# Two buffers for the offset rows, a split turn of the features, taps divided by pair, and a bank sum in one VectorE operation

## What is computed

```
off1 = make_offset(conv3x3(x, tm1_w, tm1_b), conv3x3(x, tr1_w, tr1_b))
out  = relu(batchnorm(deform_conv(x, off1, dcn1_w), bn1_g, bn1_b))
off2 = make_offset(conv3x3(out, tm2_w, tm2_b), conv3x3(out, tr2_w, tr2_b))
out  = batchnorm(deform_conv(out, off2, dcn2_w), bn2_g, bn2_b)
return relu(out + x)
```

## Time and profile before

| | |
|---|---|
| median of 3 runs | 425.51 us (425.49 to 426.92) |
| profiled execution | 425.25 us, of which the traced span is 423.4 us |
| PE busy | 395.9 us, 94% of the span |
| ACT busy | 326.9 us, 77% |
| DVE busy | 312.6 us, 74% |
| POOL busy | 105.3 us, 25% |
| granted TensorE clock | 0.99 in the mean |

### The profile page before, as it was taken

How to read it: one execution, slowest core, us unless ns; L and a number is a source line. 1 busy time by engine, 2 the same in 40 slices (tenths; PEclk the granted TensorE clock), 3 DMA queues, 4 the chain that set the end, 5 groups by cost and what they waited for, 6 DMA issues and landing times.

```text
span 423.4 us, 19117 instructions
## 1 busy us (share of the span) xinstructions
PE 395.9 (94%) x7747; PEld 354.7 (84%) x7747; DVE 312.6 (74%) x868; ACT 326.9 (77%) x423; POOL 105.3 (25%) x229
## 2 busy tenths in 40 slices
PE   4878999999999999999998899999999999999980
PEld 4666789999999999999885788999999898998870
DVE  4658977778887777777438888877777777777435
ACT  2627878888888898888836878888888889888745
POOL 6203413333333222229001422222111222220000
PEclk9999999999999999999999999999999999999996
DMA  7301422221122222222001331222222222222005
GB/s 227 80 2 36 83 56 52 49 43 35 34 41 46 45 45 45 48 50 41 2 3 26 60 65 35 50 45 45 45 45 48 47 47 48 49 49 40 4 2 198
DMA packets 61433, 21.28 MB, mean 50 GB/s; under 512 B 53702, under 2 KB 61212, under 8 KB 61388
## 3 DMA queue, kind: packets, MB, share of 16 engines
q1 hardware_dynamic: 56876, 18.34, 20.3%
q0 software_dynamic: 4512, 2.30, 2.1%
HBM read 3.23 MB, written 2.10 MB: 13 GB/s over the span
## 4 chain that ended last, share of the span: by engine, by line
PE 87%; DVE 5%; ACT 2%; DMA 2%; issue 1%; SPq 1%; DVEq 0%; ACTq 0%
PE acc_ps L759 56%; PE z_ps L732 12%; PE build_ps L717 9%; PE side_ps L665 3%; PE acc_ps L783 3%; PE side_ps L654 2%; DMA xs<-in_x 1%; ACT raw L576 1%; PE acc_ps L611 1%; PE build_ps L601 1%; DMA moved<-conv_sb 1%; DVE bstats L891 1%; PE acc_ps L643 1%; SPq L291 1%; ACT S L495 1%
## 5 line engine op out<-in xcount | busy, mean ns | idle before, releaser
L759 PE MATMUL acc_ps<-S,Z 64*64 64x256 f32 x4416 | 279.2, 377 | 1.7 <-issue 0.9
L759 PEld LDWEIGHTS acc_ps<-S,Z 64*64 64x64 f32 x4416 | 223.8, 133 | 20.8 <-issue 3.6
L495 ACT ACTIVATE S<-build_ps,minus 128x1024 f32<-128x1024 f32 x190 | 201.4, 1112 | 29.2 <-PE build_ps L717 28.9
L732 PE MATMUL z_ps<-wz,xflat 64*64 64x192 f32 x1536 | 106.7, 328 | 0.0
L717 PE MATMUL build_ps<-feat_rows,cst 64*64 64x512 f16 x576 | 82.5, 377 | 2.3 <-ACT S L495 1.2
L488 ACT ACTIVATE Z<-z_ps 128x768 f32<-128x768 f32 x96 | 78.2, 814 | 4.9 <-PE z_ps L732 4.9
L732 PEld LDWEIGHTS z_ps<-wz,xflat 64*64 64x64 f32 x1536 | 75.5, 132 | 6.7 <-issue 1.3
L1020 DVE TENSOR_SCALAR S<-build_ps 128x512 f32<-128x512 f32 x96 | 66.0, 688 | 17.3 <-PE build_ps L717 16.1
L291 POOL DMA_DIRECT2D moved<-conv_sb x128 | 64.9, 514 | 18.1 <-POOL conv_sb L384 15.8
L1022 DVE TENSOR_SCALAR S<-build_ps 128x512 f32<-128x512 f32 x96 | 65.3, 680 | 0.0
L384 POOL TENSOR_TENSOR conv_sb<-conv_sb,cst 128x32 f32<-128x32 f32 x28 | 7.5, 268 | 205.7 <-ACT conv_sb L482 205.7
(11 more groups left out here) (116 smaller groups left out, 305.1 us busy)
## 6 DMA issues: line engine op xcount, KB each, us to landing
xs<-in_x SPq DMA_DIRECT2D x4, 512.0 KB, 6.6
out<-raw SPq DMA_DIRECT2D x7, 256.0 KB, 2.5
moved<-conv_sb SPq DMA_DIRECT2D x56, 11.2 KB
moved<-conv_sb POOLq DMA_DIRECT2D x56, 11.3 KB, 1.6
moved<-conv_sb POOLq DMA_DIRECT2D x44, 11.2 KB, 1.6
wz<-in_dcn_w POOLq DMA_DIRECT2D x2, 288.0 KB, 4.7
feat_rows<-feats SPq DMA_TRANSPOSE x32, 3.7
moved<-conv_sb SPq DMA_DIRECT2D x28, 12.0 KB
```

The lines of the kernel that those rows point to most:

```text
L495: act.activation(S[:, (parity + b) % 2, half, 0:ACT_TAPS, :], build_ps[:, 0:ACT_TAPS, :], ACT.Relu, bias=minus2[:, :], scale=1.0 if half = ...
L732: mm = pe.matmul(z_ps[halves[c], i, h * BLOCK_COLS:(h + 1) * BLOCK_COLS], xflat[parity][halves[i], pixels], wz[halves[i], layer, h, b * BL ...
L759: mm = pe.matmul(acc_ps[halves[i], g, 0:HW], Z[halves[g], slot, i, half, j * C:(j + 1) * C], S[halves[g], slot, half, j, :].rearrange(by_i ...
```

## The change

Five edits, on all engines:

- `conv_sb` and `moved` become two buffers each, chosen by the pair's parity, with semaphores of their own; the waits that `shift` and `copy_taps` of pair index 3 had (`after_places`, `after_shift`) go. On ACT that `copy_taps` moves ahead of `copy_Z(T, 2)` in index 0, and `pad(T + 4)` moves behind `rectify(T, 2)`.
- The taps are divided between SP and POOL anew: of pair index 2 SP moves four and POOL five, of index 3 two and seven, of all others five and four.
- The features of the pair with index 1 are turned by two transfers, four slices and then eight, with semaphores of their own; PE's `build` of that pair's block 0 waits for the first alone, and stands after two steps of `sample(T, 0, 2)` and not after four.
- `keep_sums` on DVE is one operation, which adds `lower_sums` to `acc_ps` bank 0; `upper_kept` goes, and `sample(T, 0)` on PE waits for `raw_ready`.
- The statistics of a layer's first pair are taken in index 14 and not in index 1.

```diff
-SP_TAPS = (4, 1, 7, 3)
-POOL_TAPS = (0, 2, 5, 6, 8)
-LATE_SP_TAPS, LATE_POOL_TAPS = SP_TAPS + POOL_TAPS[4:], POOL_TAPS[:4]
-EARLY_PAIRS = 4
+TAP_ORDER = (4, 1, 7, 3, 8, 5, 6, 2, 0)
+SP_TAPS_OF_FIRST, SP_TAPS_OF_OTHERS = (4, 2), 5
...
-        conv_sb = sb("conv_sb", [P, HW])
-        moved = sb("moved", [P, HW])
+        conv_sb = [sb(f"conv_sb{i}", [P, HW]) for i in range(2)]
+        moved = [sb(f"moved{i}", [P, HW]) for i in range(2)]
...
-                turn_feats(first, 0, SLICES)
-                shift(first + 2, layer)
-                turn_feats(first + 1, 1)
+                turn_feats(first, 0, slice(SLICES, SLICE_BLOCKS))
+                shift(first + 2, 0, layer)
+                turn_feats(first + 1, 1, slice(0, SLICES), second_turned)
+                turn_feats(first + 1, 1, slice(SLICES, SLICE_BLOCKS))
...
-            def shift(T, layer, after_places=False):
+            def shift(T, parity, layer):
...
-                if after_places:
-                    pool.wait_ge(places_done, T)
-                move_taps(pool, LATE_POOL_TAPS if is_late(T, layer) else POOL_TAPS, shifted_by_pool)
+                move_taps(pool, parity, TAP_ORDER[:taps_by_sp(T, parity, layer) - 1:-1], shifted_by_pool)
...
                     rectify(T, parity, 1)
                     if index == 0:
+                        copy_taps(T + 3, 1 - parity, layer, T + 2)
                         copy_Z(T, parity, 2)
+                        rectify(T, parity, 2)
                         pad(T + 4, parity, T + 4 - first, layer)
-                        copy_taps(T + 3, layer, True)
-                        rectify(T, parity, 2)
...
                 if b == 0:
-                    wait(pe, upper_kept, T)
-                    wait(pe, lower_kept, T)
+                    wait(pe, raw_ready, T)
...
-                    places_of_taps(T + 2, layer)
-                    sample(T, 0, 2, range(4))
-                    build(T + 1, 1, 0, layer)
+                    places_of_taps(T + 2, 0, layer)
+                    sample(T, 0, 2, range(2))
+                    build(T + 1, 1, 0, layer, second=True)
                     weigh(T + 1, 1, 0, layer)
-                    sample(T, 0, 2, range(4, 6))
+                    sample(T, 0, 2, range(2, 6))
...
             def keep_sums(T, t):
                 wait(dve, sampled, BLOCKS * (T + 1))
-                dve.tensor_copy(raw[:, t, :], acc_ps[:, 0, 0:HW]).then_inc(upper_kept, 1)
-                wait(dve, upper_kept, T + 1)
                 wait(dve, lower_kept, T + 1)
-                dve.tensor_tensor(raw[:, t, :], raw[:, t, :], lower_sums[:, :], ALU.add).then_inc(raw_ready, 1)
+                dve.tensor_tensor(raw[:, t, :], acc_ps[:, 0, 0:HW], lower_sums[:, :], ALU.add).then_inc(raw_ready, 1)
...
-                    statistics(T - 1, T - 1 - first)
+                    if index != 1:
+                        statistics(T - 1, T - 1 - first)
+                    if index == PAIRS - 2:
+                        statistics(first, 0)
```

More of the change, by code:

```diff
@@ L284, in program, with move_taps @@
         turned_ps = (acc_ps[:, 0, 0:2 * P], acc_ps[:, 1, 0:2 * P])
-        def move_taps(eng, taps, shifted):
+        def move_taps(eng, parity, taps, shifted):
             for k in taps:
@@ L416, in body @@
                     if index < PAIRS - 3:
-                        shift(T + 3, layer, index == 0)
+                        shift(T + 3, 1 - parity, layer)
                     if 0 < index < PAIRS - 2:
@@ L538, in _ @@
                 rectify_first_half(first)
-                copy_taps(first + 2, layer)
+                copy_taps(first + 2, 0, layer)
                 rectify(first, 0, 0, (1,))
@@ L700, in places, with build @@
                 mm.then_inc(places_done, 1)
-            def build(T, parity, b, layer, is_first=False, products=range(6)):
+            def build(T, parity, b, layer, is_first=False, products=range(6), second=False):
                 if products[0] == 0:
@@ L707, in build @@
                         wait(pe, rows_by_dve, layer + 1)
-                    elif b == (1 if is_first else 0):
+                    elif b == 0 and second:
+                        wait(pe, second_turned, 16 * (layer + 1))
+                    elif b == (1 if is_first or second else 0):
                         wait(pe, feats_turned, turned(T))
@@ L836, in body @@
                         conv_taps(T + 3, 1 - parity, layer, T + 1)
-                    build(T, parity, 1, layer, products=range(4))
+                    build(T, parity, 1, layer, products=range(4), second=index == 1)
                     if index is None or index < PAIRS - 2:
-                        places_of_taps(T + 2, layer)
+                        places_of_taps(T + 2, parity, layer)
                     build(T, parity, 1, layer, products=range(4, 6))
@@ L996, in features @@
                             wait(dve, first_turned, layer + 1)
+                        if isinstance(T, int) and T == layer * PAIRS + 2:
+                            wait(dve, second_turned, 16 * (layer + 1))
                         ins = dve.tensor_tensor(taken[:, :, :, ROW_CODES],
```

114 lines of the change are left out of this document (58 added, 56 removed).

## The result

The changed kernel takes 431.99 us in the median of six runs (431.37 to 434.65), the kernel before 425.87 us on the same chip (six runs). The ratio of the two is 1.0141, with a 95% interval of 1.0107 to 1.0175: about 6.0 us slower (4.6 to 7.5). The forecast was 3.8 us slower. Two executions count as slow and stand outside the ratios of this document: one of the kernel before at 430.68 us, beside `raw_last` and `stats_early`, and one of `kept_last` at 1921.63 us.

The account below looks back on a forecast made before the run. PE, busy 395.9 of 423.4 us, was taken to bound the kernel. Loop pairs 4.0, written-out pairs 1.0 and layer start -1.2 gave +3.8 us: 429.3 us, forecast band 427.5 to 431.5, range 424.2 to 435.0.

Parts of the forecast that it names:

- Loop pairs: Heads of the twenty loop pairs: PE's sampling starts later behind the one-operation sum, 0.2 us a pair, +4.0 us (0 to +8.0).
- the last quarter would sample from 96.25 to 96.33 and lose 0.07 to 0.15: Odd loop pair's head: PE's last quarter, free of weighing at 96.18, waits for the load at 96.25.
- Written-out pairs: Eight pairs, indices 12 to 15 of each layer: 0.05 us for 12 and 13, 0.2 for 14 and 15, +1.0 us.
- Start of a layer: Second pair's sampling starts earlier, limited by DVE's features: -0.98 us in layer 1, -0.2 in layer 0, together -1.2.
- Statistics, tap shares, second buffers at nothing: Moved statistics, new SP and POOL shares, and extra loads and memset at the program's head were forecast to cost nothing.
- Rival 1: At pair heads the whole array waits for the first product: 0.40 us a loop pair, +10.0, 435.5 us; chance 0.22.
- Rival 2: The wait at pair heads is absorbed: -1.2, 424.3 us, chance 0.14; 423.5 and below, chance 0.06.
- Rival 3: Layer start gains nothing, as POOL's taps land late or two transfers hold SP up: +5.0, 430.5 us; chance 0.08.
- the spacing: Sign: equal pieces of PE's chain of waits lie 11.3 to 11.6 us a pair apart instead of 11.24.
- the earlier second sampling: Sign: PE's first sampling product of the second pair comes about 1 us earlier in layer 1, about 0.2 in layer 0.
- The addition's delay of 0.04 to 0.13 us: Sign: DVE's addition starts that long after the end of ACT's `lower_sums`.
- PE's list of waits: Sign: PE waits for DVE's `raw` line, 0.1 to 0.3 us each, some 30 times.

Follow-up runs that it names:

- raw_last: Changed kernel without VectorE's redundant wait for the sampling, and TensorE waits for Z and S first, the sum last: 429.69 us, ratio to before 1.0080.
- stats_early: Changed kernel with the first pair's statistics put back to the second pair: 433.46 us, ratio to before 1.0165.
- kept_last: `two_ops` with TensorE waiting for Z and S first and for the two bank copies last: 425.72 us, ratio to before 0.9983.
- bank1_first: Changed kernel with a pair's first sampling product taken on bank 1 ahead of bank 0, bank 1 waiting for ScalarE's copy alone: 432.60 us, ratio to before 1.0121.
- one_wait_less: Changed kernel without VectorE's own wait for the sampling ahead of the addition: 431.35 us, ratio to before 1.0143.
- one_op_alone: Kernel before with the bank sum in one operation and nothing else of the change: 433.24 us, ratio to before 1.0189.
- sum_twice: Changed kernel with the bank sum's addition made twice in a row, TensorE waiting for the second: 446.12 us, ratio to before 1.0446.
- two_ops: Changed kernel with the bank sum put back to two operations, copy then addition, all else kept: 424.57 us, ratio to before 0.9987.

## Why the prediction was right, and where its sizes were not

The sign and the range held; the forecast's own band, 427.5 to 431.5 us, was just missed, since the loss was larger than forecast. Term by term, beside the 7.0 us of the stage table:

- **Loop pairs: forecast +4.0 (0 to 8.0), measured +6.1.** The mechanism, a price near what the last quarter loses, is what `bank1_first` and the table of quarters show. The step that was mis-sized is "the last quarter would sample from 96.25 to 96.33 and lose 0.07 to 0.15": it lost 0.22 us in this odd pair (1.11 to 1.33) and 0.32 in an even one (1.03 to 1.35); the pairs lost 0.24 and 0.34. Three things went into it. The addition came 0.21 to 0.23 us behind the copy, not 0.13: I took the delay of a wait on one of two inputs from the earlier trace rows, and the new wait stands with a second one ahead of an operation whose address is made in the loop (`one_wait_less` takes 0.07 off). PE's step was 0.21, a little under my 0.25. And from the first product to the last quarter's start it is another 0.07 us, which I left out. I also read the last quarter's freedom in the odd pair alone; in the even one it had begun earlier.
- **Written-out pairs: forecast +1.0, measured +1.7.** Index 12 lost 0.04 (forecast 0.05), index 14 0.26 (forecast 0.2: its last quarter started at 0.86 before and at 1.13 after). The rest is index 13: it took 10.94 us before and 11.28 after, though its last quarter started at 1.11 and 1.13. I put it with 12 and measured it by its last quarter; but in it the first two quarters count, and those went from 0.78 to 1.12, just the 0.34 that the pair lost.
- **Start of a layer: forecast -1.2, measured -0.85** (way to head 1 and pair 1 together: -0.16 in layer 0, -0.69 in layer 1). My figure held the new sum at head 1, and so does this one. The mechanism came: what is late next is DVE with the features of pair index 2, the addition of head 1 starts 0.64 us behind ACT's copy, and PE waits 0.27 us for it. That PE samples 0.98 us earlier in layer 1 and 0.2 in layer 0 came out as 1.3 and 0.4, reckoned from each layer's start. What I left out is what pair 1 gives back behind that: 0.57 us in layer 1 and 0.29 in layer 0, from its first sampling product to head 2; the unnamed stall in layer 0 is 0.49 us where it was 0.29, and one of 0.18 us came in layer 1; the rest is open. Beside the one-operation sum the other parts are worth 1.9 us by the stage table (`one_op_alone` against the changed kernel; 2.0 by their times), of which 0.68 is a difference in layer 1's way to head 1 that single executions can't tell; beside two operations they are worth some 0.5.
- **Statistics, tap shares, second buffers at nothing:** no row speaks against it for the statistics and the loop's shares. At the start of layer 0 PE now waits 0.33 us for the shifted rows of pair index 3, where it had not waited before; the last of SP's two taps landed at 49.28 and of POOL's seven at 49.09. Shares and buffers were not tried alone.
- **Rivals.** Rival 1 at 0.40 a pair: falls with `bank1_first`, although the total lies between it and the forecast. Rival 2: falls with `sum_twice` and `one_op_alone`. Rival 3: both waits of the earlier trace rows are gone in the changed kernel, but the 0.8 us hung on a late landing, and `two_ops` has waits of 0.47 and 0.72 us for the shifted rows at the same places of the two layers; so it falls beside the one-operation sum only, and beside two operations most of it holds.

Of the signs I had named, the spacing (11.50 and 11.56 us, within 11.3 to 11.6) and the earlier second sampling came. The addition's delay of 0.04 to 0.13 us was wrong in the loop (0.21 to 0.23), a wait for `moved` remained, and PE's list of waits did not show the wait some 30 times but twice; a sign that can be read only in the timeline was the wrong one to name. No version beat the kernel before by more than the uncertainty: `two_ops` and `kept_last` are 0.1 to 0.2% ahead, with 1.0 at the edge of both intervals.

## What to carry to other kernels

An operation saved on an engine that waits saves nothing; if the saving turns two parallel releases into a chain, the whole chain is paid at every place where the next engine has no slack. On an array split in quarters, look for the quarter whose work ends last, which here was mostly the one that starts last, and measure the new chain against that one, for every parity of the loop and every kind of pair. And price a chain by its waits as well as by its operations: here 0.42 us of addition came with 0.42 us of steps between engines, and in the loop these cost twice what they cost in written-out code.

## What the runs showed of the hardware

- Between engines, in the loop against written-out code: ACT's end to DVE's start 0.21 to 0.23 us against 0.10, DVE's end to PE's load 0.21 against 0.12. One redundant wait on DVE was worth 0.07 us in both, but nothing in the odd loop pairs of layer 1.
- The order of waits ahead of one instruction changes its response to the last of them, and not always for the better: with the late one last, PE's load came 0.07 us behind it in the loop instead of 0.21, but 0.23 instead of 0.12 in written-out code.
- Quarters of the array are independent to the end: a quarter that starts 0.23 us earlier than in the changed kernel (188.90 against 189.34, each from its head) does nothing for the pair.
- The Trainium skill, page "VectorE: DVE Perf Modes", section "Rules for kernel authors", advises against fusing chained operations for speed, and a smaller count of operations rather than of semaphores. Here one operation of two was saved and the kernel became 1.9% slower (`one_op_alone`), because the chain that counted ran over three engines.
